# Where ScalarE saves the end state of a scan: ahead of the decay of its tile, and by itself for five units that GpSimd weighs

## The reference, cut to what matters

```python
dA = jnp.exp(dt[..., None] * A)
dBx = (dt * xi)[..., None] * Bm[:, :, None, :]
def step(h, inp):
    a, bx, c = inp
    h = a * h + bx
    return (h, jnp.einsum('bds,bs->bd', h, c))
```

## Time and profile before

| what | value |
|---|---|
| median of 3 runs | 4715.81 us (4712.54 to 4718.79) |
| the profiled execution | 4716.4 us |
| its span, first to last instruction | 4714.5 us |
| mean granted TensorE clock | 0.984 |
| Mamba phase, about | 74 to 3400 us of the span |
| feed-forward phase, about | 3400 us to the end |

### The profile page before, as it was taken

How to read it: one execution, slowest core, us unless ns; L and a number is a source line. 1 busy time by engine, 2 the same in 40 slices (tenths; PEclk the granted TensorE clock), 3 DMA queues, 4 the chain that set the end, 5 groups by cost and what they waited for, 6 DMA issues and landing times. The chain is left out here.

```text
span 4714.5 us, 67115 instructions
## 1 busy us (share of the span) xinstructions
PE 4468.1 (95%) x24932; PEld 3384.7 (72%) x24932; DVE 3889.1 (82%) x4136; ACT 3105.2 (66%) x5147; POOL 3319.4 (70%) x1559
## 2 busy tenths in 40 slices
PE   8999999999999999999999999998799999999999
PEld 3676666667666666766666776666588888888888
DVE  6999999999999999999999999999754544444442
ACT  6777777777777777777777777777344444444443
POOL 5999999999999999999999999999620000000000
PEclk9999999999999999999999999999899999999999
DMA  8545544444554445454444455445220101110100
GB/s 295 173 138 151 143 139 139 138 145 135 153 141 141 140 133 139 136 150 137 137 139 133 134 144 141 136 134 178 99 92 23 41 28 36 32 36 32 36 23 10
DMA packets 297736, 545.76 MB, mean 116 GB/s; under 512 B 101888, under 2 KB 186624, under 8 KB 262784
## 3 DMA queue, kind: packets, MB, share of 16 engines
q1 hardware_dynamic: 296512, 529.91, 38.1%
q10 hardware_dynamic: 896, 11.54, 0.7%
HBM read 502.77 MB, written 50.14 MB: 117 GB/s over the span
## 5 line engine op out<-in xcount | busy, mean ns | idle before, releaser
L1425 DVE TENSOR_TENSOR_SCAN m_h<-bank,m_state,m_dBx 128x512 f32<-128x512 f32 x1512 | 1838.6, 1268 | 39.2 <-ACT bank L1167 27.8
L884 PEld LDWEIGHTS bank<-ident,m_h 128*128 128x128 f32 x8192 | 974.0, 143 | 533.1 <-issue 372.4
L884 PE MATMUL bank<-ident,m_h 128*128 128x128 f32 x8192 | 1211.5, 277 | 75.5 <-DVE m_h L1433 62.9
L1308 POOL TENSOR_TENSOR m_dBx<-u,m_Bs 128x1024 f32<-128x1024 f32 x432 | 1017.8, 2380 | 1.0 <-DVE m_h L1425 0.9
L1308 POOL TENSOR_TENSOR m_dBx<-m_u,m_Bs 128x1024 f32<-128x1024 f32 x432 | 1016.2, 2374 | 0.0
L1319 POOL TENSOR_TENSOR m_h<-m_h,m_Cs 128x1024 f32<-128x1024 f32 x384 | 909.9, 2370 | 70.7 <-ACT m_state L1099 64.3
L1433 DVE TENSOR_TENSOR m_h<-m_h,bank 128x1024 f32<-128x1024 f32 x640 | 769.6, 1202 | 15.6 <-PE bank L866 13.5
L1167 ACT ACTIVATE bank<-m_dt,cols 128x512 f32<-128x512 f32 x864 | 586.2, 689 | 222.2 <-DVE m_h L1425 219.3
L1167 ACT ACTIVATE bank<-dt,cols 128x512 f32<-128x512 f32 x864 | 585.4, 689 | 189.8 <-DVE m_h L1425 186.7
L303 POOL TENSOR_TENSOR mvj<-mvj,norm_c 128x4 f32<-128x4 f32 x16 | 16.5, 1033 | 970.6 <-DVE mvj L264 970.6
L866 PEld LDWEIGHTS bank<-ident,m_Ct 128*128 128x128 f32 x2560 | 303.7, 138 | 347.7 <-issue 188.8
(11 more groups left out here) (186 smaller groups left out, 5829.7 us busy)
## 6 DMA issues: line engine op xcount, KB each, us to landing
m_Bs<-b_dram SPq DMA_DIRECT2D x256, 1024.0 KB, 5.8
m_Cs<-c_dram SPq DMA_DIRECT2D x384, 256.0 KB, 3.6
m_dg<-d_dram SPq DMA_DIRECT2D x160, 256.0 KB, 3.9
xx<-in_x SPq DMA_DIRECT2D x16, 512.0 KB, 5.9
xn_dram<-xx SPq DMA_DIRECT2D x16, 512.0 KB, 3.2
yb_dram<-m_ysb SPq DMA_DIRECT2D x16, 512.0 KB, 3.3
xx<-xn_dram SPq DMA_DIRECT2D x16, 512.0 KB, 3.8
x_dram<-m_ysb SPq DMA_DIRECT2D x16, 512.0 KB, 3.3
```

The source lines that it names most:

```text
L884: mm = pe.matmul(YB[b][:, o:o + P], h[:, k % NH, m, tok:tok + P], ident[:, :], start=(s == 0 and o == 0), stop=False, is_transpose=True, s ...
L1308: pool.tensor_tensor(dBx[:, dbx_ring(ch, k) % NDBX, :, :], u[ch.batch][:, m, :], Bs[:, k // BP % 2, k % BP, :].unsqueeze(1).broadcast_to(( ...
L1425: dve.tensor_tensor_scan(o, decays, share, initial, ALU.mult, ALU.add).then_inc(S["scan"], 1)
```

## The change

It moves `keep_state` ahead of the decay, at every even step k for unit k/2 - 2, and it gives the even units 2, 16, 18, 20 and 22 (`SAVE_ONE`, the even ones among `P_UNITS`) a copy of their own; their odd neighbours then copy one unit instead of two. All other odd units copy the pair, as before. A chunk has 21 copies instead of 16. Each copy waits for exactly the scans that it reads, and the waits for `save` of GpSimd and VectorE count the new copies.

```diff
+SAVE_ONE = (2, 16, 18, 20, 22)
+SAVES = tuple(k for k in range(32) if k % 2 or k in SAVE_ONE)
+NSAVE = len(SAVES)
...
+        def saved(k):
+
+            return sum(j < k for j in SAVES) + 1
...
-            def keep_state(ch, p):
-
-                k = 2 * p
-                act.wait_ge(S["scan"], ch.at(STEPS, 2 * k + 4))
-                act.copy(state[:, ch.batch, k:k + 2, :], h[:, k % NH:k % NH + 2, :, 0 if rev(ch) else T - 1]
+            def keep_state(ch, k):
+                if k not in SAVES:
+                    return
+                a = k if k % 2 == 0 or k - 1 in SAVE_ONE else k - 1
+                act.wait_ge(S["scan"], ch.at(STEPS, 2 * k + 2))
+                act.copy(state[:, ch.batch, a:k + 1, :], h[:, a % NH:k % NH + 1, :, 0 if rev(ch) else T - 1]
                          ).then_inc(S["save"], 1)
...
                 for k in range(STEPS):
+                    if k % 2 == 0:
+                        old = unit(ch, k // 2 - 2)
+                        if old:
+                            keep_state(*old)
                     decay(ch, k)
...
-                    if k % 4 == 2:
-                        old = unit(ch, (k - 6) // 2)
-                        if old:
-                            keep_state(old[0], old[1] // 2)
...
-                keep_state(ch, DS - 1)
+                for k in (NU - 2, NU - 1):
+                    keep_state(ch, k)
...
-                pool.wait_ge(S["save"], ch.at(DS, k // 2 + 1))
+                pool.wait_ge(S["save"], ch.at(NSAVE, saved(k)))
...
-                dve.wait_ge(S["save"], ch.at(DS, k // 2 + 1))
+                dve.wait_ge(S["save"], ch.at(NSAVE, saved(k)))
```

## The result

The changed kernel takes 4728.4 us (median of 12 runs, 4724.7 to 4732.2); the kernel before, timed beside it, takes 4715.8 us (12 runs). The ratio is 1.0029, with a 95% interval from 1.0020 to 1.0037: slower by 0.3%. Forecast were 4731 us and a ratio of 1.0032. The profiled execution took 4731.1 us, with a span of 4729.3 us, against a span of 4714.5 before: 14.8 us more.

What follows compares the result with a forecast made beforehand. VectorE was taken to set the pace in steady chunks, with ScalarE's late decays, and GpSimd only at the pass switch. 4716.4 + 18.3 - 1.7 - 1.3 = 4731.7, less 0.6 for the median: 4731 us; range 4711 to 4739.

Steps and rivals of the forecast that it cites:

- GpSimd's waits, at nothing: Steady chunks: GpSimd's waits for saved state, up to 52.5 us, shrink, but nobody waits for GpSimd, so no time gained.
- The rival that GpSimd was the bound: Whole kernel: VectorE is held by dBx through waits filed elsewhere, so 52.5 us come off, 4663 us; chance 0.05.
- Step 44, +0.61 us in 30 chunks: ScalarE: unit 20's copy waits for scan 41, delaying evacuation, TensorE, dt product and tile 53's decay: +18.3 us.
- The wait I had announced as 0.6: VectorE, ahead of tile 53: a new wait of some 0.6 us for its decay, as a sign in the changed profile.
- Switch of passes, -1.74: Between passes: GpSimd's lead, cut at 2.35 us by unit 27's copy, less 0.61 us of late ScalarE, shortens VectorE's waits.
- the sentence that the DMA queues move only with GpSimd: DMA queues: C and B rows are asked for up to 3 us sooner, which delays nobody.
- Tile 24 of pass 2, -1.3: ScalarE, pass 2: a copy moved into its wait for TensorE brings tile 24's decay 0.09 us sooner in some 14 chunks.
- The copies' own work, at nothing: ScalarE: five more copies a chunk, each delaying a decay by 0.09 us, hidden by slack; at 0.19 us, 2 us.
- The cover: Step 44: the evacuation does not really release TensorE, or a link has slack, so 4712 us; chance 0.28.

Runs made afterwards that it cites:

- the first experiment: Changed kernel, with the copy of unit 20 at step 44 put behind the decay and the evacuation of YB: 4711.2 us, ratio 0.9992.
- The last experiment: Changed kernel, with only the load of the seventh B row put ahead of the store of y in SyncE's queue: 4727.9 us, ratio 1.0030.
- the five versions: Changed kernel with: no unit 20 copy; that copy behind evacuation; that plus B row first; no SAVE_ONE copies; evacuation ahead of copy. 4710.7 to 4715.3 us.

## Why the prediction was right

**GpSimd's waits, at nothing.** Right. They fell by 37.5 us and the chunk did not shorten by anything, with the loss or, in the first experiment, without it (103.19 against 103.18 us). The rule of the Trainium skill that I had set against this (Perfetto Trace Analysis, Optimizing Scalar/DVE Operations: broken up instructions may let work be done sooner) holds here in its wording and not in its hope. In chunk 12 of the changed kernel GpSimd weighs unit 16 without a wait, 18.98 us behind the scan of tile 24, where it was 21.98 before: 3.0 us sooner, as forecast. Five dBx later it waits for a B row:

```profile
1373.12 2.36 POOL L1328 TENSOR_TENSOR m_h<-m_h,m_Cs 128x1024 f32<-128x1024 f32 x1
...
1396.24 2.37 POOL L1317 TENSOR_TENSOR m_dBx<-u,m_Bs 128x1024 f32<-128x1024 f32 x1 [2.16 <-DMA m_Bs<-b_dram]
```

The rival that GpSimd was the bound (4663 us) is out.

**Step 44, +0.61 us in 30 chunks.** Right in mechanism, link by link, and a little high in size. The shift along the chain is 0.63 to 0.66 us, a chunk loses 0.59. The wait I had announced as 0.6 reads as 0.39 in the row, because two scans in a row overlap: in the kernel before they start 1.19 us apart and take 1.28. The start of scan 53 is 1.67 us behind that of scan 52, so 0.48 is lost there, and 0.08 more ahead of tile 52. For the same reason, and for the gain at tile 24, VectorE's waits for decays rose by 9.8 us only and not by 17. What failed in this term is the count. In chunks 1, 16 and 17 the scan of tile 53 waits 0.45 us for its decay already in the kernel before; chunks 0 and 1 together lost 0.2 us, chunks 16 and 17 some 0.33 each, and the full amount was lost in chunks 2 to 15 and 18 to 30. One of these 27, chunk 14, is the one that goes into the switch. That leaves 26 x 0.59 + 0.9 = 16.2 us and not 18.3. The prediction calls that chunk the last one of pass 1; it is the last but one. VectorE's three waits "at the switch" lie at tiles 8, 12 and 14 of chunk 15, the last of pass 1, where GpSimd makes the diagonals.

**Switch of passes, -1.74.** It came to -0.99. The failed step is the sentence that the DMA queues move only with GpSimd and that the earlier requests delay nobody. B row 7 of a chunk is loaded behind the store of y, and this store waits for a tanh of ScalarE that step 44 has made late. GpSimd in the changed kernel, just ahead of the switch:

```profile
1601.54 2.38 POOL L1317 TENSOR_TENSOR m_dBx<-u,m_Bs 128x1024 f32<-128x1024 f32 x1 [1.13 <-DMA m_Bs<-b_dram]
...
1613.98 2.35 POOL L1317 TENSOR_TENSOR m_dBx<-m_u,m_Bs 128x1024 f32<-128x1024 f32 x1 [0.66 <-DMA m_Bs<-b_dram]
```

The second wait lies behind the weighing of unit 27, which the save bounds, and counts in full: 0.99 + 0.66 = 1.65, which is the forecast but for 0.1. The last experiment took it away and got 0.63 back. I had followed GpSimd's and ScalarE's own order, and for the queue only what moves sooner in it, not what a late store holds up.

**Tile 24 of pass 2, -1.3.** Right: its wait is 0.54 us, against 0.64 in the earlier trace rows, and a chunk of pass 2 lost 0.49 us (102.56 against 102.07) where one of pass 1 lost 0.59. The gain of 0.1 us shows in 16 chunks and not in 14, which makes -1.6.

**The copies' own work, at nothing.** Right: 16 or 21 copies, ahead of the decays or behind, left the chunk at 103.2 us.

**The sum.** Of the span's +14.8 us, some 15.0 are the chunks (with the gain at tile 24 in it) and -1.0 the switch. The rest is not the change's, or was not foreseen: a prologue that ran 1.9 us shorter, a disturbance of about 1.7 us that shows once in the trace of before and twice in this one, and 1.0 us more in the last chunk, where GpSimd waits for its C row behind the load of the feed-forward weights. By the medians the change costs 12.7 us, where 15 were forecast; the terms as measured give 16.2 - 1.0 - 1.6 = 13.6. That the profiled span is 14.8 us longer, so near the forecast, is in part luck. The cover that I gave 0.28 to does exist, as a number: the time of that rival, 4712 us, is what the changed kernel takes with the one copy out of the way (4710.7 and 4711.2).

**What stays open.** Whether the early copies gain anything that the time can show. The traces have a gain: with them and without the late evacuation a chunk of pass 2 takes some 101.99 us and not 102.07, and the stretch with the switch (tile 24 of chunk 14 to tile 24 of chunk 15) 107.5 to 109.2 us and not 109.8. But the five versions lie at 4710.7, 4711.2, 4711.3, 4714.4 and 4715.3 us, each interval reaches 1, and the distance is under the 0.2% that I set. The experiments act on the wait and on the evacuation; the links behind it, from TensorE to the scan of tile 53, are read from the traces, and no run moves one of them alone. The 1.7 us disturbance was not looked into.

## What to carry to other kernels

An instruction moved ahead on an in-order engine brings its wait along; cost the wait by what stands behind it on that engine, and follow this from link to link until one has slack, rather than by the length of the instruction itself (0.19 us here, for a loss of 0.59 us a chunk). Idle time of an engine that nobody waits for is no reserve of time: remove its cause and it comes back under another name. A join that starts right at its release pays for lateness and gives nothing for earliness (0.61, 0.65 and 0.66 us late cost 0.52, 0.57 and 0.58 us a chunk in three versions; 0.61 us early gave none), so before putting anything ahead of it, look whether it can stand behind.

## What the runs showed that was not expected

A lateness does not always come out where a smaller one did. At 0.6 us VectorE lost 0.59 us a chunk, ahead of tiles 52 and 53; with the evacuation 2.91 us late it lost most of the time at an earlier tile, of which TensorE makes the input. And a stall can cost more than its length: behind the same stall of TensorE a chunk lost 2.85 us where the clock stayed full, and 4.2 to 4.5 us where the granted clock was half. A wait that a row shows is less than what the wait costs where two instructions overlap otherwise: 0.39 us shown and 0.48 lost between two scans. And a store of y in SyncE's queue, though it has nothing to do with the rows of B, made GpSimd wait for them once GpSimd was ahead: 12.1 us with the store in time (the first experiment), 44.3 us with the store 0.66 us late and the copies as changed.
